# A mixture of experts with two results per token: numbering and loading them in a low and a high block, with VectorE adding x and the high result

## The chip, the cores and the metric

One core of a Trainium2 chip (trn2). A time is the device time of one execution in microseconds; a version is judged by the median of its runs. Engines: PE is TensorE (PEld its weight loads), DVE is VectorE, ACT is ScalarE, POOL is GpSimd, SP is SyncE, which only issues transfers here. An engine's own instruction queue is written SPq, POOLq and so on.

## What is computed

`x` is 2048 tokens of 128 features in float32. The block is a "macaron": half a mixture-of-experts FFN, a causal linear attention, and the same FFN again.

```python
x = x + 0.5 * ffn(layernorm(x))
x = x + attention(layernorm(x))
x = x + 0.5 * ffn(layernorm(x))

def ffn(x):                                   # 8 experts, the best 2 for each token
    top_w, top_i = top_k(x @ Wg, 2)
    top_w = softmax(top_w)
    for i in range(8):                        # w[..., i] is top_w where i was chosen, else 0
        h = gelu(x @ W1[i] + b1[i])           # 128 -> 512
        results += w[..., i] * (h @ W2[i] + b2[i])
```

## The kernel before

**Tiles.** The 2048 tokens are NT = 16 tiles of 128, handled at the end of each FFN in NC = 4 chunks of CH = 4 tiles. Each token has two results, so an FFN has 4096 of them, in NL = 32 tiles of 128 "slots". Slots are sorted by expert, and within an expert by token tile. A tile that two experts share is computed once for each, so an FFN works through NS = 39 items. The program does everything twice where a helper has the argument `f` (0 for the first FFN, 1 for the second), with the attention between.

**Routing (L758 to L924).** VectorE ranks the eight logits of each token, counts the tokens of each expert and gives each of a token's two choices its slot (`picked`, `pos_i`, L803 to L806), the first half of `pos_i` for the best expert (rank 0) and the second for the next (rank 1). From that TensorE builds two tables by slot: `src_row`, the token that a slot belongs to, and `pair_row` (L870), the row of the DRAM tensor `y_rows` in which the slot's result goes: two times the token plus the rank. The weights of the two ranks are `half_w`. Last on VectorE in this stage comes `landed_no` (L916 to L924): for the chunks 0 to 2, up to which count each of four scatter semaphores must have come so that all results of the chunk have been scattered. EARLY = 3 is the number of these chunks.

**Experts.** For each item TensorE computes the hidden layer (L1156) and, one item later, the output (L1165); ScalarE does the gelu (L626) and VectorE the masked sum into `y_back` (L941). GpSimd gathers the rows of each slot tile (L465) and, eight items behind, scatters each finished tile to `y_rows` (L482), on four semaphores in turn; a scatter waits for the one four before it.

**SyncE in an FFN (L336 to L373).** Its queue is in this order: the normalized rows to DRAM (L347), the 39 loads of the first layer's weights as their buffers come free (L355), then for the chunks 0 to 2 twelve reads of `landed_no` into registers (L367), and last, for each chunk, four waits on scatters (L371) and one load of 512 KB from `y_rows` into `y_back` (L372). A chunk's load waits only for the scatters up to its own last result; the last chunk waits for all.

**The end of an FFN.** TensorE puts into a PSUM bank for each chunk the bias (`mix_bias`, L1199), then x by an identity matmul for each tile (`mix_start`, L1204), then the rank-0 results by a matmul with a diagonal matrix of their weights (`mix`, L1129; the diagonals come from ScalarE during the experts, L631). A `mix` waits for the chunk's load. TensorE does the `mix_start` of chunk c + 1 ahead of the `mix` of chunk c; the last `mix` comes after the first tile of the attention has been turned and projected. VectorE (`combine`, L977) adds the bank and the rank-1 results with their weights into x, chunk by chunk. In the first FFN it takes each chunk's moments (L971) and, after chunk 0, the variance; GpSimd computes the root (L492), VectorE the shift (L753, after chunk 1), ScalarE normalizes the first tile of the attention (`xa`, L665), TensorE turns and projects it (L1251, L1259). The first prefix matmul (L1283) comes behind eight warming matmuls (L1062) and writes the banks 0 to 2, so it also waits for all of `combine`. In the second FFN SyncE stores each chunk of x to the output (L377).

```python
landed = [[sp.value_load(landed_no[P - 1:P, c, r:r + 1], ...) for r in range(LANDED)] for c in range(EARLY)]   # L367
for c in range(NC):
    for r in range(LANDED):
        sp.wait_ge(scattered[r], landed[c][r] if c < EARLY else 16 * (NL // LANDED) * (f + 1))                 # L371
    sp.dma_start(y_back[:, c * CH:(c + 1) * CH, :, :], back_rows[:, c * CH:(c + 1) * CH, :, :])                # L372
```

Of the kernel before, what the change touches and what calls it, by code (L numbers as in the profile page):

```python
# [27 lines left out]
P = 128  # L28
# [10 lines left out]
def macaron_kernel(nc, x_d, xT_d, Wa, ba, Wg, W1b, W2, b2, out_d):  # L39
# [38 lines left out]
    EARLY = T // P // 4 - 1  # L78
    assert D == P and NS % RING == 0 and WEIGHTS % RING == 0 and WEIGHTS % ACTS == 0 and T & (T - 1) == 0

    with ExitStack() as ctx:
# [95 lines left out]
        last_slot = sb("last_slot", [P, EARLY])  # L177
        landed_sum = sb("landed_sum", [P, EARLY, LANDED], I32)
        landed_no = sb("landed_no", [P, EARLY, LANDED], I32)
        residue = sb("residue", [P, EARLY, LANDED])  # L180
# [5 lines left out]
        picked = sb("picked", [P, TOPK, NT, E])  # L186
# [22 lines left out]
        y_back = sb("y_back", [P, NT, TOPK, P])  # L209
        xg = y_back[:, :, :, :].rearrange("p t k d -> p (t k) d")  # L210
        y_sum = y_back[:, :, :, :].rearrange("p t k d -> p (t k d)")
# [58 lines left out]
        y_loaded = [sem(f"y_loaded{c}") for c in range(NC)]  # L270
# [22 lines left out]
        def mix_bank(c): return banks[:, (1, 2, 0, 3)[c], :]  # L293
# [31 lines left out]
        def _(sp):  # L325
# [10 lines left out]
            for f in range(2):  # L336
# [25 lines left out]
                for i in range(NS // WEIGHTS * WEIGHTS, NS):  # L362
                    stage(i, i % WEIGHTS)
                back_rows = y_rows[f].rearrange("(p t k) d -> p t k d", k=TOPK, p=P)

                sp.wait_ge(landed_ready, f + 1)
                landed = [[sp.value_load(landed_no[P - 1:P, c, r:r + 1], min_val=16, max_val=32 * NL // LANDED)  # L367
                           for r in range(LANDED)] for c in range(EARLY)]
                for c in range(NC):
                    for r in range(LANDED):  # L370
                        sp.wait_ge(scattered[r], landed[c][r] if c < EARLY else 16 * (NL // LANDED) * (f + 1))  # L371
                    sp.dma_start(y_back[:, c * CH:(c + 1) * CH, :, :],  # L372
                                 back_rows[:, c * CH:(c + 1) * CH, :, :]).then_inc(y_loaded[c], 16)  # L373
# [8 lines left out]
        def _(pool):  # L382
# [25 lines left out]
            g.iota(residue[:, :, :], pattern=[[0, EARLY], [-P, LANDED]], base=4 * P - 1, channel_multiplier=0, **flt).then_inc(consts, 1)  # L408
# [158 lines left out]
        def _(act):  # L567
            s = nc.scalar

            def ffn(f):  # L570
# [59 lines left out]
                def weights(t):  # L630
                    s.activation(diag[:, t, :], ident[:, :], ACT.Copy, scale=half_w[:, 0, t:t + 1]).then_inc(diag_ready, 1)  # L631
# [7 lines left out]
                act.wait_ge(half_ready, f + 1)  # L639
# [85 lines left out]
        def _(dve):  # L725
# [32 lines left out]
            def gate_and_route(f):  # L758
# [35 lines left out]
                if f == 0:  # L794
# [8 lines left out]
                link(v.tensor_tensor(picked[:, :, :, :], is_rank[:, :, :, :],  # L803
                                     slot[:, :, :].unsqueeze(1).to_broadcast([P, TOPK, NT, E]), ALU.mult))
                with nc.allow_low_precision(reason="whole numbers below 2 ** 24, summed in float32"):
                    link(v.tensor_reduce(pos_i[:, :], picked[:, :, :, :].rearrange("p k t e -> p (k t) e"),  # L806
                                         AX.X, ALU.add))
# [47 lines left out]
                for k in range(3, len(HOTS[f])):  # L855
# [14 lines left out]
                v.scalar_tensor_tensor(out=pair_row[:, :], in0=src_row[:, :], scalar=float(TOPK),  # L870
                                       in1=back_bank[:, NL:2 * NL], op0=ALU.mult, op1=ALU.add).then_inc(pair_ready, 1)
# [44 lines left out]
                v.tensor_tensor(last_slot[:, :], slot[:, CH - 1:EARLY * CH:CH, E - 1], chosen[:, CH - 1:EARLY * CH:CH, E - 1],  # L916
                                ALU.add).then_inc(last_ready, 1)
                dve.wait_ge(last_ready, 2 * f + 1)
                v.scalar_tensor_tensor(out=landed_sum[:, :, :], in0=last_slot[:, :].unsqueeze(2).to_broadcast([P, EARLY, LANDED]),
# [46 lines left out]
            def combine(f):  # L966
# [5 lines left out]

                for c in range(NC):
                    dve.wait_ge(mix_ps, NC * f + c + 1)
                    dve.wait_ge(y_loaded[c], 16 * (f + 1))
# [79 lines left out]
        def _(pe):  # L1055
# [77 lines left out]
            def experts(f):  # L1133
# [85 lines left out]
                for c in range(NC):  # L1219
                    mix_bias(c)  # L1220
# [144 lines left out]
```

## Time and profile before

| | us |
|---|---|
| median of 3 runs | 310.52 (310.47 to 310.52) |
| the profiled execution | 308.35 |
| its span, first to last instruction | 306.2 |
| PE busy | 275.5 (90%) |
| DVE busy | 163.3 (53%) |
| ACT busy | 176.4 (58%) |
| POOL busy | 194.9 (64%) |
| mean granted TensorE clock | 0.937 |

The profiled execution has 2.15 us around its span. All start times in the rows are from the span's start. By stages: up to about 30 us the loads and the routing of the first FFN, from 30 to 106 its experts, to about 122 its end, to 195 the attention, to 214 the second routing, to 291 the second experts, and to 306 the end. Register reads, waits and the issue of a transfer are not counted as busy; they show only where one asks for their line.

### The profile page before, as it was taken

Reading aid. Unit: us, or ns where it says so; the run is one execution under the profiler, and the core shown is the slowest. Engines: PE = TensorE matmul, PEld = TensorE weight load, DVE = VectorE, ACT = ScalarE, POOL = GpSimd, SP = SyncE. Lnnn points to the kernel's source line nnn. Section 1 sums busy time; section 2 is a strip of 40 time slices with the busy share of each in tenths; the row PEclk is TensorE's granted clock in tenths of the full one; section 3 lists DMA queues with packets and bytes.
Section 4 is the critical chain, followed back from the end, with each engine's and each line's share of the span. In section 5 each row is a group of like instructions: output and inputs, shape, how many; then the busy total and the mean of one; then the engine's idle time right before and its main releaser. Section 6 shows DMA issues by size and latency. Waiting matters only on the chain.

```text
span 306.2 us, 8012 instructions
## 1 busy us (share of the span) xinstructions
PE 275.5 (90%) x2028; PEld 236.2 (77%) x2033; DVE 163.3 (53%) x557; ACT 176.4 (58%) x643; POOL 194.9 (64%) x256
## 2 busy tenths in 40 slices
PE   8765999999999968989999999576999999999964
PEld 5432999999999956657777776433899999999954
DVE  1789222222222237799999999999222232222214
ACT  2793488887676603353555463384488887676400
POOL 7234777777777622786678878244777777776620
PEclk9576699999999999999999999776699999999999
DMA  5983767666675172000000000021866767675175
GB/s 176 307 273 94 223 190 198 187 193 192 192 213 163 47 230 104 1 0 2 0 2 3 0 0 36 1 104 55 236 188 190 192 191 190 200 208 160 47 255 183
DMA packets 22407, 41.53 MB, mean 136 GB/s; under 512 B 3937, under 2 KB 5985, under 8 KB 22370
## 3 DMA queue, kind: packets, MB, share of 16 engines
q1 hardware_dynamic: 18274, 32.68, 36.5%
q0 software_dynamic: 4096, 8.40, 9.0%
q8 instruction: 19, 0.31, 0.4%
q14 instruction: 18, 0.15, 0.1%
HBM read 33.72 MB, written 7.34 MB: 134 GB/s over the span
## 4 chain that ended last, share of the span: by engine, by line
PE 61%; DVE 12%; DMA 10%; issue 5%; POOL 5%; ACT 4%; SPq 1%; DVEq 0%; POOLq 0%; ACTq 0%
PE banks L1156 22%; PE banks L1165 20%; PE banks L1283 5%; DMA y_back<-y_rows 3%; PE banks L1173 3%; PE banks L1259 2%; DVE prod L1006 2%; DVE local L1010 2%; POOL y_rows L482 2%; DMA x<-in_x_tiles 2%; DMA y_back<-xn_rows,src_row 2%; ACT diag L582 2%; POOL kv L505 2%; PE banks L1285 2%; ACT rows_sb L588 1%
## 5 line engine op out<-in xcount | busy, mean ns | idle before, releaser
L626 ACT ACTIVATE h_act<-banks,w1b 128x128 f32<-128x128 f32 x312 | 89.1, 376 | 12.3 <-PE banks L1156 12.3
L1156 PE MATMUL banks<-rows_sb,w1b 128*128 (+1 forms) x624 | 87.0, 285 | 1.2 <-ACT rows_sb L609 1.2
L941 DVE SCALAR_TENSOR_TENSOR y_back<-banks,own_item,y_back 128x128 f32 x78 | 27.4, 351 | 110.2 <-PE banks L1165 110.2
L465 POOL DMA_INDIRECT y_back<-xn_rows,src_row x64 | 61.6, 963 | 32.4 <-issue 15.9
L1165 PE MATMUL banks<-w,h_act 128*128 (+1 forms) x624 | 81.8, 275 | 0.0
L1156 PEld LDWEIGHTS banks<-rows_sb,w1b 128*128 128x128 f32 x624 | 79.8, 200 | 2.1 <-issue 2.0
L482 POOL DMA_INDIRECT y_rows<-y_back,pair_row x64 | 62.7, 980 | 22.5 <-issue 11.9
L1165 PEld LDWEIGHTS banks<-w,h_act 128*128 128x128 f32 x624 | 75.6, 192 | 0.0
L505 POOL TENSOR_TENSOR kv<-qk,vx 128x1024 f32<-128x1024 f32 x16 | 31.5, 1969 | 16.4 <-DVE qk L963 16.4
L609 ACT COPY rows_sb<-banks 128x128 f32<-128x128 f32 x64 | 16.5, 266 | 34.8 <-PE banks L1173 34.0
L1283 PE MATMUL banks<-kv,tri 128*128 128x384 f32 x64 | 24.8, 510 | 2.0 <-POOL kv L505 2.0
L1006 DVE TENSOR_TENSOR prod<-banks,qk 128x1152 f32<-128x1152 f32 x16 | 21.6, 1352 | 2.8 <-PE banks L1287 2.7
L1010 DVE TENSOR_REDUCE local<-prod 128x144 f32<-128x1152 f32 x16 | 21.6, 1353 | 0.5
L1062 PE MATMUL banks<-blank 128*128 128x512 bf16 x52 | 18.4, 502 | 2.6 <-DVE blank L994 1.2
L1173 PE MATMUL banks<-ident,y_back 128*128 128x128 f32 x64 | 17.9, 292 | 2.6 <-DMA y_back<-xn_rows,src_row 1.9
L931 DVE TENSOR_TENSOR y_back<-blank 128x128 bf16 (+1 forms) x64 | 18.2, 284 | 0.0
L1283 PEld LDWEIGHTS banks<-kv,tri 128*128 128x128 f32 x64 | 10.9, 189 | 9.1 <-POOL kv L505 4.2
L675 ACT ACTIVATE neg<-banks 128x256 f32<-128x256 f32 x16 | 6.1, 383 | 18.7 <-PE banks L1259 18.7
L977 DVE SCALAR_TENSOR_TENSOR x<-y_back,half_w,banks 128x128 f32<-128x128 f32 x32 | 8.9, 343 | 13.9 <-PE banks L1129 13.9
L1062 PEld LDWEIGHTS banks<-blank 128*128 128x128 bf16 x57 | 6.6, 125 | 10.9 <-issue 6.8
L688 ACT COPY mT<-banks 128x128 f32<-128x128 f32 x16 | 4.2, 265 | 18.3 <-PE banks L1264 18.3
L665 ACT ACTIVATE xa<-x,shift,rstd 128x128 f32<-128x128 f32 x16 | 8.0, 507 | 10.7 <-DVE shift L756 10.7
(207 smaller groups left out, 403.0 us busy)
## 6 DMA issues: line engine op xcount, KB each, us to landing
w1b<-in_W1b SPq DMA_DIRECT2D x78, 258.0 KB
y_back<-y_rows SPq DMA_DIRECT2D x8, 512.0 KB, 5.0
xn_rows<-rows_sb SPq DMA_DIRECT2D x8, 256.0 KB, 2.4
rows_sb<-in_x_T SPq DMA_DIRECT2D x4, 256.0 KB, 4.1
x<-in_x_tiles SPq DMA_DIRECT2D x4, 256.0 KB, 6.6
y_back<-xn_rows,src_row POOLq DMA_INDIRECT x64, 3.4
y_rows<-y_back,pair_row POOLq DMA_INDIRECT x64
out<-x SPq DMA_DIRECT2D x4, 256.0 KB, 2.3
```

Source lines behind the costliest of these rows:

```text
L465: g.indirect_dma_start(out=xg[:, n, :], out_offset=None, in_=xn_rows[f][:, :], in_offset=bass.IndirectOffsetOnAxis(ap=src_row[:, n:n + 1], ...
L482: g.indirect_dma_start(out=y_rows[f][:, :], out_offset=bass.IndirectOffsetOnAxis(ap=pair_row[:, i:i + 1], axis=0), in_=xg[:, i, :], in_off ...
L505: g.tensor_tensor(o4, k4, v4, ALU.mult).then_inc(kv_sb, 1)
L626: ins = s.activation(h_act[:, i % ACTS, c * P:(c + 1) * P], h_bank(i % RING)[:, c * P:(c + 1) * P], ACT.Gelu_apprx_tanh, bias=w1b[:, i % W ...
L941: v.scalar_tensor_tensor(out=total, in0=y_bank(r), scalar=own_item[:, bass.ds(i, 1)], in1=total, op0=ALU.mult, op1=ALU.add).then_inc(y_sb, 1)
L1006: v.tensor_tensor(prod[:, :].rearrange("p (b e n) -> p b e n", b=3, n=P), prefix_bank.rearrange("p b (e n) -> p b e n", n=P), q4, ALU.mult ...
L1010: v.tensor_reduce(local[:, :, :].rearrange("p e h -> p (e h)"), prod[:, :].rearrange("p (g d) -> p g d", d=DH), AX.X, ALU.add).then_inc(lo ...
L1062: mm(banks[:, bank, :], blank[:, 0:P], blank[:, :], start=True, stop=True)
L1156: last = mm(h_bank(r)[:, c * P:(c + 1) * P], w1b[:, q, c * P:(c + 1) * P], xgT[:, bass.ds(at[i][0], P)], start=True, stop=True)
L1165: last = mm(y_bank(r), h_act[:, a, c * P:(c + 1) * P], w2[:, bass.ds(col + c * P, P)], start=(c == 0), stop=(c == FC - 1))
L1173: pe.transpose(xg_bank(n), xg[:, n, :], ident[:, :]).then_inc(xg_ps, 1)
L1283: mm(prefix_bank[:, b, :], tri[:, :], kv[:, r, b * n:(b + 1) * n, :].rearrange("p e n -> p (e n)"), start=True, stop=True)
```

## The change

A token's two results are told apart by the number of the expert, no longer by rank. "High" is the one with the larger slot (the higher expert), "low" the other. `y_rows` becomes two blocks of 2048 rows, first all low results, then all high ones; `pair_row` is 2048 times the side plus the token. Since slots are sorted by expert, a low result is never of expert 7 and a high one never of expert 0.

- The positions: `picked` is made once for both choices; the high slot is its maximum, the low slot its sum less that.
- New on VectorE, behind the routing: masks of the two sides, and from them `side_w`, the weights by side (in place of `half_w` in the combine and in ScalarE's diagonals, which now wait for `side_ready`). `last_slot` has the last slot of expert 6 and of expert 7 for each chunk, `landed_no` 8 x 4 counts in place of 3 x 4.
- SyncE reads 16 counts, issues four loads of the low block (256 KB each), reads 12 more counts, and issues four loads of the high block.
- The identity matmuls are gone. VectorE adds x to each bank in one operation over 128x512, once TensorE has written the biases of all four (`bias_ps`); TensorE's `mix` of the low results waits for that (`x_added`) and for the low load; the combine adds the high results.
- All four `mix` come at the end of the experts, the last one no longer behind the first tile of the attention.

```diff
                 sp.wait_ge(landed_ready, f + 1)
-                landed = [[sp.value_load(landed_no[P - 1:P, c, r:r + 1], ...)
-                           for r in range(LANDED)] for c in range(EARLY)]
+                low = [landed_counts(0, c) for c in range(NC)]
                 for c in range(NC):
-                    for r in range(LANDED):
-                        sp.wait_ge(scattered[r], landed[c][r] if c < EARLY else 16 * (NL // LANDED) * (f + 1))
-                    sp.dma_start(y_back[:, c * CH:(c + 1) * CH, :, :], ...).then_inc(y_loaded[c], 16)
+                    load_side(0, c, low[c], low_loaded[c])
+                high = [landed_counts(1, c) for c in range(NC - 1)] + [[16 * (NL // LANDED) * (f + 1)] * LANDED]
+                for c in range(NC):
+                    load_side(1, c, high[c], high_loaded[c])
...
+                def load_side(k, c, landed, loaded):
+                    for r in range(LANDED):
+                        sp.wait_ge(scattered[r], landed[r])
+                    sp.dma_start(y_back[:, k, c * CH:(c + 1) * CH, :],
+                                 back_rows[:, k, c * CH:(c + 1) * CH, :]).then_inc(loaded, 16)
+                def landed_counts(k, c):
+                    return [sp.value_load(landed_no[P - 1:P, c * SIDES + k, r:r + 1], ...) for r in range(LANDED)]
...
-                link(v.tensor_tensor(picked[:, :, :, :], is_rank[:, :, :, :], slot[...].to_broadcast([P, TOPK, NT, E]), ALU.mult))
-                    link(v.tensor_reduce(pos_i[:, :], picked[...], AX.X, ALU.add))
+                link(v.tensor_tensor(picked[:, :, :], chosen[:, :, :], slot[:, :, :], ALU.mult))
+                    v.tensor_reduce(pos_i[:, NT:], picked[:, :, :], AX.X, ALU.max).then_inc(dve_step, 1)
+                    link(v.tensor_reduce(both_pos[:, :], picked[:, :, :], AX.X, ALU.add))
+                link(v.tensor_tensor(pos_i[:, 0:NT], both_pos[:, :], pos_i[:, NT:], ALU.subtract))
...
+                link(v.tensor_tensor(is_side[:, 1, :, :], picked[:, :, :], pos_i[:, NT:]..., ALU.is_equal))
+                link(v.tensor_tensor(is_side[:, 0, :, :], chosen[:, :, :], is_side[:, 1, :, :], ALU.subtract))
+                dve.wait_ge(w_all_ready, f + 1)
+                link(v.tensor_tensor(side_pair[:, :, :, :], is_side[:, :, :, :], w_all[...]..., ALU.mult))
+                v.tensor_reduce(side_w[...], side_pair[...], AX.X, ALU.add).then_inc(side_ready, 1)
...
+                dve.wait_ge(bias_ps, f + 1)
+                for c in range(NC):
+                    v.tensor_tensor(mix_bank(c), mix_bank(c), x[:, c * CH:(c + 1) * CH, :]..., ALU.add).then_inc(x_added, 1)
+                dve.wait_ge(side_ready, f + 1)
                 for c in range(NC):
                     dve.wait_ge(mix_ps, NC * f + c + 1)
-                    dve.wait_ge(y_loaded[c], 16 * (f + 1))
+                    dve.wait_ge(high_loaded[c], 16 * (f + 1))
...
             def mix(f, c):
-                pe.wait_ge(y_loaded[c], 16 * (f + 1))
+                pe.wait_ge(low_loaded[c], 16 * (f + 1))
+                pe.wait_ge(x_added, NC * f + c + 1)
...
-                mix_start(0)
+                last.then_inc(bias_ps, 1)
                 pe.wait_ge(diag_ready, NT * (f + 1))
-                for c in range(1, NC):
-                    mix_start(c)
-                    mix(f, c - 1)
+                for c in range(NC):
+                    mix(f, c)
```

## Rows read from the trace of the kernel before

**Rows 1.** The chain that ended last, end of the first FFN: start us, us, what

```profile
110.30 4.31 DMA y_back<-y_rows
...
117.34 0.50 ACT xa L665
...
123.72 1.29 PE banks L1283 x4
```

**Rows 2.** The same chain, end of the second FFN

```profile
290.64 2.23 DMA y_rows<-y_back,pair_row
...
302.72 0.78 DVE x L977 x3
```

**Rows 3.** L367 on SyncE's queue by FFN: count, ns min/median/max, first and last start

```profile
L367 SPq TENSOR_LOAD <-landed_no x12: 272/278/398, 94.9 to 101.4; - x12
...
L367 SPq TENSOR_LOAD <-landed_no x12: 272/279/412, 278.7 to 285.1; - x12
```

**Rows 4.** SyncE's loads of y_back: timeline of 109 to 111, then L372 in all

```profile
110.30 0.81 SPq L372 DMA_DIRECT2D y_back<-y_rows  x2
...
L372 SPq DMA_DIRECT2D y_back<-y_rows x8: 319/328/1607, 106.0 to 295.9; - x8
```

**Rows 5.** Timeline of GpSimd: scatter of tile 27 (first FFN), tile 28 (second)

```profile
102.04 0.97 POOL L482 DMA_INDIRECT y_rows<-y_back,pair_row  x1 [0.30 <-DVE y_back L941]
...
287.58 0.97 POOL L482 DMA_INDIRECT y_rows<-y_back,pair_row  x1 [0.42 <-DVE y_back L941]
```

**Rows 6.** The page's transfers: count, KB each, median us from issue to landing

```profile
xn_rows<-rows_sb SPq DMA_DIRECT2D x8, 256.0 KB, 2.4
```

**Rows 7.** Timeline of VectorE and GpSimd, end of the first FFN

```profile
111.23 1.12 DVE L977 SCALAR_TENSOR_TENSOR x<-y_back,half_w,banks 128x128 f32<-128x128 f32 x4 [4.14 <-PE banks L1129]
...
114.36 1.05 POOL L492 TENSOR_TENSOR rstd<-var,minus_half 128x4 f32<-128x4 f32 x1 [5.28 <-DVE var L748]
...
115.85 1.12 DVE L977 SCALAR_TENSOR_TENSOR x<-y_back,half_w,banks 128x128 f32<-128x128 f32 x4 [1.57 <-PE banks L1129]
```

**Rows 8.** Timeline of TensorE's bias matmuls; L1006 on VectorE (ns min/median/max)

```profile
106.53 1.14 PE L1199 MATMUL banks<-b_blk,w_allT 32*128 32x512 f32 x8
...
290.32 1.14 PE L1199 MATMUL banks<-b_blk,w_allT 32*128 32x512 f32 x8
...
L1006 DVE TENSOR_TENSOR prod<-banks,qk x16: 1339/1356/1358, 125.7 to 191.1; 128x1152 f32<-128x1152 f32 x16
```

**Rows 9.** Stretches: length, busy PE, PEld, DVE, ACT, POOL, granted clock, DMA, GB/s

```profile
113.00:114.00 1.00, 0.00 (x0) 0.00 (x0) 0.90 (x8) 0.00 (x0) 0.00 (x0) 1.00 1.01 389
192.00:196.00 4.00, 1.15 (x8) 0.59 (x7) 3.83 (x12) 0.99 (x4) 0.02 (x1) 0.99 0.01 2
196.00:197.00 1.00, 1.00 (x4) 0.91 (x4) 0.99 (x8) 0.10 (x1) 0.00 (x0) 0.50 0.00 0
30.00:35.00 5.00, 4.29 (x18) 3.90 (x19) 1.59 (x7) 1.75 (x7) 3.78 (x5) 0.50 0.91 261
35.00:36.00 1.00, 1.00 (x9) 1.00 (x8) 0.00 (x0) 0.50 (x3) 0.69 (x2) 0.75 0.69 118
```

**Rows 10.** TensorE at either clock: projection, a matmul of its shape, warming matmuls

```profile
118.64 0.91 PE L1259 MATMUL banks<-w_fold,xaT 128*128 128x384 f32 x2 [0.35 <-ACT xaT L672]
...
13.94 1.65 PE L1089 MATMUL banks<-w_attn,center 128*128 128x384 f32 x2
...
L1062 PE MATMUL banks<-blank x7: 379/379/379, 122.0 to 123.3; 128*128 128x512 bf16 x7
...
L1062 PE MATMUL banks<-blank x4: 634/634/634, 200.9 to 202.1; 128*128 128x512 bf16 x4
```

**Rows 11.** Timeline of VectorE: the positions in the second routing

```profile
201.42 0.67 DVE L803 TENSOR_TENSOR picked<-is_rank,slot 128x256 f32<-128x256 f32 x1
202.12 0.42 DVE L806 TENSOR_REDUCE pos_i<-picked 128x32 int32<-128x256 f32 x1
```

**Rows 12.** Timeline of VectorE: its first output of the second experts

```profile
221.37 0.35 DVE L941 SCALAR_TENSOR_TENSOR y_back<-banks,own_item,y_back 128x128 f32 x1 [5.23 <-PE banks L1165]
```

More of the change, by code:

```diff
@@ L176, in macaron_kernel @@
         place = sb("place", [P, NS, 2], I32)
[L177 to L180, printed above, removed]
+        last_slot = sb("last_slot", [P, NC, SIDES])
+        landed_sum = sb("landed_sum", [P, NC * SIDES, LANDED], I32)
+        landed_no = sb("landed_no", [P, NC * SIDES, LANDED], I32)
+        residue = sb("residue", [P, NC * SIDES, LANDED])
         expert_i = sb("expert_i", [P, NS], I32)
@@ L185, in macaron_kernel @@
         slot = sb("slot", [P, NT, E])
-        picked = sb("picked", [P, TOPK, NT, E])
+        picked = sb("picked", [P, NT, E])
+        both_pos = sb("both_pos", [P, NT], I32)
+        is_side = sb("is_side", [P, SIDES, NT, E])
+        side_pair = sb("side_pair", [P, SIDES, NT, E])
+        side_w = sb("side_w", [P, SIDES, NT])
         pos_i = sb("pos_i", [P, TOPK * NT], I32)
@@ L269, in macaron_kernel @@
         y_ps, y_sb = map(sem, ("y_ps", "y_sb"))
-        y_loaded = [sem(f"y_loaded{c}") for c in range(NC)]
+        low_loaded = [sem(f"low_loaded{c}") for c in range(NC)]
+        high_loaded = [sem(f"high_loaded{c}") for c in range(NC)]
+        bias_ps, x_added = sem("bias_ps"), sem("x_added")
+        side_ready = sem("side_ready")
         xa_sb, xa_ps, xaT_sb, qkv_ps = map(sem, ("xa_sb", "xa_ps", "xaT_sb", "qkv_ps"))
@@ L638, in ffn @@
                 step(2)
-                act.wait_ge(half_ready, f + 1)
+                act.wait_ge(side_ready, f + 1)
                 for t in range(NT):
@@ L869, in gate_and_route @@
                 dve.wait_ge(table_ready, f + 1)
-                v.scalar_tensor_tensor(out=pair_row[:, :], in0=src_row[:, :], scalar=float(TOPK),
-                                       in1=back_bank[:, NL:2 * NL], op0=ALU.mult, op1=ALU.add).then_inc(pair_ready, 1)
+                v.scalar_tensor_tensor(out=pair_row[:, :], in0=back_bank[:, NL:2 * NL], scalar=float(T),
+                                       in1=src_row[:, :], op0=ALU.mult, op1=ALU.add).then_inc(pair_ready, 1)
                 dve.wait_ge(item_step, done[0])
@@ L1126, in mix @@
             def mix(f, c):
-                pe.wait_ge(y_loaded[c], 16 * (f + 1))
+                pe.wait_ge(low_loaded[c], 16 * (f + 1))
+                pe.wait_ge(x_added, NC * f + c + 1)
                 for t in range(c * CH, (c + 1) * CH):
-                    last = mm(mix_bank(c)[:, (t % CH) * P:(t % CH + 1) * P], diag[:, t, :], y_back[:, t, 0, :],
+                    last = mm(mix_bank(c)[:, (t % CH) * P:(t % CH + 1) * P], diag[:, t, :], y_back[:, 0, t, :],
                               start=False, stop=True, skip_group_check=True)
@@ L1198, in mix_bias @@
                     rows = slice(c * CH * E, (c + 1) * CH * E)
-                    mm(mix_bank(c), w_allT[rows, :], b2_blk[rows, :], start=True, stop=False, skip_group_check=True)
-                def mix_start(c):
-                    for t in range(c * CH, (c + 1) * CH):
-                        mm(mix_bank(c)[:, (t % CH) * P:(t % CH + 1) * P], ident[:, :], x[:, t, :],
-                           start=False, stop=False, skip_group_check=True)
+                    return mm(mix_bank(c), w_allT[rows, :], b2_blk[rows, :], start=True, stop=False, skip_group_check=True)
                 step(0)
@@ L1312, in _ @@
             project(0)
-            mix(0, NC - 1)
             turn_x(1)
@@ L1327, in _ @@
             experts(1)
-            mix(1, NC - 1)
 _INS = ['x_tiles', 'x_T', 'W_attn', 'b_attn', 'L0_ffn_Wg', 'W1b', 'L0_ffn_W2', 'b2_blk']
```

40 lines of the change are left out of this document (22 added, 18 removed).

## The prediction

> **What bounds the kernel now.** I read the chain of waits first, at the ends of the two FFN stages, because everything the change moves lies there. At the end of the first FFN the chain goes through a load of y_back that takes 4.31 us after its issue at 110.30, and then reaches the first normalized tile of the attention (xa at 117.34) and the first prefix matmul (123.72) [rows 1]. At the end of the second it goes through the landing of a scatter (2.23 us), a load and the last additions on VectorE, which end at 302.72 + 0.78 = 303.50 [rows 2]. So both ends hang on when the y_back loads are issued and how long they take. SyncE issues them, so I looked next at what SyncE itself does: its register reads of landed_no, which the page counts in no busy time. There are twelve per FFN; in the first they start from 94.9 to 101.4, one every (101.4 - 94.9) / 11 = 0.59 us, in the second from 278.7 to 285.1, one every 0.58 us [rows 3]. In the kernel before they are hidden: the first load can't be issued before tile 28 or 29 of the results has landed anyway.
>
> **The change part by part.** *SyncE.* The twelve reads become 28: sixteen ahead of the low loads and twelve more between the low loads and the high loads. SyncE does one thing after another, so the high loads are queued behind all 28, and VectorE's combine waits for them. Two loads without a wait are issued 0.81 - 0.33 = 0.48 us apart (two of them span 0.81, the median of one is 0.33) [rows 4].
>
> First FFN: sixteen reads from 94.9 end at 94.9 + 16 x 0.59 = 104.3. The low loads need tiles 24, 25, 26 and 27 (my count of the given inputs' routing: the last expert-6 row of each chunk of four token tiles; the high loads need 28, 29, 30, 31). Tile 27 is scattered at 102.04 [rows 5] and lands 2.2 us later, at 104.2. So all four low loads go out at once, 104.4 to 106.3. Twelve reads more: 106.3 + 7.1 = 113.4. The high loads follow at 113.45, 113.9, 114.4 and 114.9, although the last scatter has landed by 110.3. A high load is 256 KB. The rows have 2.4 us for 256 KB in the other direction [rows 6] and 4.31 for 512 KB in this one, the first of three in a row [rows 1]. I take 2.7, near the row of equal size, and keep 2.4 and 4.3 as ends. Chunk 0 is then there at 116.15. In the kernel before its additions start at 111.23, and the way from there over the moments to GpSimd's root ends at 114.36 + 1.05 = 115.41, after 4.18 us [rows 7]; xa followed only at 117.34, since VectorE did chunk 1 in between (115.85 + 1.12 = 116.97) and then two small operations, some 0.4 us. After the change chunk 1 fits under those 4.18 us. So the root ends at 116.15 + 4.18 = 120.33, and xa starts some 0.4 us later, at 120.75: 3.4 us later than 117.34.
>
> Second FFN: sixteen reads from 278.7 end at 278.7 + 9.3 = 288.0. The low loads need tiles 24, 25, 27, 28, the high ones 29, 30, 30, 31. Tile 28 is scattered at 287.58 [rows 5] and lands at 289.8. The last low load is issued then, SyncE is free at 290.2, twelve reads take 7.0, and the high loads start at 297.25. Chunk 0 is there at 299.95, and VectorE needs 16 x 0.26 = 4.2 us for the four chunks (one every (1.12 - 0.34) / 3 us; four take 1.12 [rows 7]). It ends at 304.2 against 303.50: 0.7 us later. The output store behind it is unchanged.
>
> *TensorE and VectorE.* The 16 identity matmuls that added x go, and VectorE adds x to the four banks instead, as soon as TensorE has written the bias: at 106.53 + 1.14 = 107.7, and at 290.32 + 1.14 = 291.5 [rows 8]. An operation over 128x1152 with one input in PSUM takes 1.36 us [rows 8]; for 128x512 that is 0.6 us, for four 2.4 to 2.7. They end at 110.3 and 294.1, before any high load is there, so they cost nothing; without that cover they would cost 2.5 us in each FFN. The mix matmuls are done about 111.3 and 295 and leave the chain.
>
> *The clock.* In the first FFN TensorE then has nothing to do from about 111.3 until the transpose of xa at 121.4. In the kernel before that stretch was filled with mixes. The granted clock stayed at 1.00 where that stretch still had a hole (113 to 114: 0.00 busy); after 192 to 196, in which TensorE was busy for 1.15 us of 4, it stood at 0.50, which is 1.2 GHz; in the first experts it stood at 0.50 from 30 to 35 though TensorE was busy for 4.29 us of these 5, and rose between 35 and 36 [rows 9]. So I expect the attention to begin at 1.2 GHz. What lies on its way to the first prefix matmul then: the two projections, 0.91 at the full clock and 1.65 for the same shape at half (+0.75 each); eight warming matmuls, starting every 0.21 us at the full clock, every 0.4 at half (+1.6); two transposes (+0.2 each) [rows 10]. Together 3.5 us, and about 2.4 more if the first prefix (2 us of matmuls) still runs slow. Ends: 0 and 5.9. I take the middle, 3.0, since the rise should fall somewhere among the warming matmuls.
>
> *Edits at little or nothing.* The positions: picked is 128x128 instead of 128x256 (0.67), and the one reduction of 0.42 becomes two of half the size and a subtraction over 16 columns [rows 11]. I reckon 1.0 in place of 1.1, that is 0, between -0.3 and +0.3; in the first FFN it is hidden behind ScalarE's squares. The new side weights add five VectorE operations, some 1.6 us, ahead of the experts. Behind them stand VectorE's first clear and output, and ScalarE's wait for side_ready stands ahead of its fourth item. VectorE idles 5.23 us before its first output at 221.37 [rows 12], and ScalarE comes to its wait later still; if that cover were gone, 1.6 us would be lost in each FFN. Scatters that meet low loads land later, but GpSimd waits only for the fourth scatter back, 4 x 1.27 = 5.1 us [rows 5], against a landing of 2.2.
>
> *Sum:* 3.4 + 3.0 + 0.7 = 7.1 us. The profiled execution took 308.35 (span 306.2 and 2.15 around it), so 315.45 there; the median of the runs is 310.52, 2.17 above it, and becomes 317.6.
>
> The Trainium skill, in "Runtime: NRT & Kernel Launch", section "Instruction fetch mechanics", gives about 200 ns for one TENSOR_LOAD of a register. Here the load alone has a median of 278 ns, and a whole read (with its check) 0.58. With 0.2 us for a read, the 28 would take 5.6 us instead of 16.4, and the time would be that of rival B.
>
> **Rivals.** *A: the clock stays up.* For it: the hole at 113 to 114 passed without a fall. Against it: the new one is four times as long as that hole in whole (some 2.5 us), and 192 to 196, with more work in it, ended in a fall. Then 310.52 + 4.1 = 314.6.
>
> *B, faster: the reads don't hold the high loads up.* The point from which it decides: without the clock the reads cost 3.4 + 0.7 = 4.1 us in all, over 28 + 12 reads that the high loads wait for, so 0.1 less for a read, 0.48 us, would make the ends even; below that the change wins. Or SyncE would have to do them earlier. Then the high loads leave with the scatters (about 106, and 295 for the last), VectorE starts on chunk 0 when its additions of x end at 110.2 instead of 111.23, chunk 1 isn't in the way of xa (114.85 instead of 117.34: -2.5), and the second FFN ends 4.2 us after 294.1, at 298.3 instead of 303.5 (-5.2). That gives 302.8. Against it: 24 reads of the same form in the trace, all at 0.58 to 0.59.
>
> *C, slower still:* four loads issued at once can hold SyncE (one of the eight took 1.6 us to issue [rows 4]), the high loads may need 4.3 us to land, and the prefix may still run at 1.2 GHz. With the clock's 5.9 and 1.6 more at each end it is 310.5 + 3.4 + 5.9 + 0.7 + 3.2 = 323.7; I don't expect all of it at once.
>
> **How the numbers follow.** The forecast 0.62; A 0.17; B, or half of it, 0.12; C beyond 321.5 0.09. The range runs from 313.5 (A with landings of 2.4 us) to 321.5 (the forecast with most of C); B is left out, as is the end of C. Faster by over 0.2% (about what a measurement of this kernel can tell) holds B: 0.11; within 0.2%, a B that breaks even, 0.03; slower 0.86.
>
> **What would show it.** Right: 28 reads at 0.58 us; the first high load issued near 113.5 and 297.2; xa near 120.75; the granted clock at 0.50 about 118 to 126; the last scatter landed some 3 us before the first high load. Wrong: the high loads issued within 1 us of their scatters (B), or a clock of 1.00 through the gap (A). If VectorE's additions of x were what its first chunk waits for, the reads would not matter.

## The result, and the profile after

The changed kernel takes 320.22 us (319.07 to 321.77, four runs) against 310.50 (310.03 to 310.52) of the kernel before on the same chip: 1.0324 times as long, interval 1.0283 to 1.0365. The prediction said 317.6, with a range of 313.5 to 321.5. The profiled execution took 321.77, with a span of 320.0.

The chain that ended last, the change's first end. It answers to [rows 1]. SPq is SyncE's queue, L381 is the line of its register reads and L377 that of its loads of y_back:

```profile
103.75 2.20 DMA y_rows<-y_back,pair_row
106.00 0.33 SPq L377
...
107.84 0.28 SPq L381
...
114.78 0.15 SPq L381
...
115.16 3.25 DMA y_back<-y_rows
118.53 1.14 DVE x L1008 x4
...
123.21 0.50 ACT xa L682
...
132.97 1.29 PE banks L1308 x4
```

Between the last low load (107.48) and the first high load (115.16) stands one read after another. Before, this place in the chain held only a load. The same chain at the second end, answering to [rows 2]:

```profile
298.24 4.31 DMA y_rows<-y_back,pair_row
302.56 0.32 SPq L377
...
302.93 0.34 SPq L381
...
309.85 3.06 DMA y_back<-y_rows
313.03 1.01 DVE x L1008 x4
...
315.98 1.29 DVE x L1008 x5
```

Here SyncE first waits for a scatter (4.31 us), then sends the last low load, then reads for 6.9 us. In the share of the chain by engine, SPq was 1% of the span before and is 4% here, and DMA went from 10% to 7%: the chain's wait has moved from transfers to the queue that issues them.

The reads and loads in all (count, ns min/median/max, first and last start), and the landing of the loads, answering to [rows 3, 4]:

```profile
L381 SPq TENSOR_LOAD <-landed_no x56: 272/276/359, 96.7 to 309.2; - x56
...
L377 SPq DMA_DIRECT2D y_back<-y_rows x16: 319/320/344, 106.0 to 311.3; - x16
...
DMA to landing us min/median/max: 3.1/3.8/4.3
```

VectorE and TensorE around the bias of the first FFN, by their timelines, answering to [rows 7, 8]:

```profile
108.28 1.14 PE L1231 MATMUL banks<-b_blk,w_allT 32*128 32x512 f32 x8
109.49 2.49 DVE L1001 TENSOR_TENSOR banks<-banks,x 128x512 f32<-128x512 f32 x4 [0.66 <-PE banks L1231]
110.33 3.81 PE L1161 MATMUL banks<-y_back,diag 128*128 128x128 f32 x32 [0.92 <-DVE banks L1001]
118.53 1.12 DVE L1008 SCALAR_TENSOR_TENSOR x<-y_back,side_w,banks 128x128 f32<-128x128 f32 x4 [6.54 <-DMA y_back<-y_rows]
```

The additions of x end at 111.98 and the mixes at 114.14, and then both engines wait for a high load. What the clock did meanwhile (stretch and length in us, busy PE, PEld, DVE, ACT, POOL, granted clock, DMA share, GB/s), answering to [rows 9]:

```profile
117.00:118.00 1.00, 0.00 (x0) 0.00 (x0) 0.00 (x0) 0.00 (x0) 0.00 (x0) 1.00 0.83 227
118.00:120.00 2.00, 0.00 (x0) 0.00 (x0) 1.44 (x6) 0.00 (x0) 0.00 (x0) 0.80 1.01 364
120.00:124.00 4.00, 0.16 (x1) 0.18 (x1) 3.70 (x21) 0.79 (x2) 1.05 (x1) 0.50 0.14 53
124.00:128.00 4.00, 2.45 (x5) 1.03 (x5) 2.56 (x11) 1.36 (x6) 0.27 (x1) 0.50 0.01 2
128.00:132.00 4.00, 4.00 (x10) 1.57 (x10) 2.83 (x15) 1.39 (x5) 2.94 (x3) 0.50 0.02 6
132.00:134.00 2.00, 2.00 (x7) 1.21 (x6) 0.00 (x0) 0.00 (x0) 2.00 (x2) 0.79 0.00 0
```

TensorE's granted clock goes from 1.00 (2.4 GHz) to 0.50 (1.2 GHz) during the wait, and the attention begins at 0.50.

For a comparison by stages I take these marks from each trace: the first bias matmul of each FFN, xa, the first prefix matmul, and the end of VectorE's last addition. The table has the differences between them in us. The ratio is the time against the kernel before on the same chip; the runs came from several chips, so kernels are compared by their ratios. The experiments are told below.

| kernel | bias 1 at | bias 1 to xa | xa to prefix | prefix to bias 2 | bias 2 to end | ratio |
|---|---|---|---|---|---|---|
| before | 106.53 | 10.81 | 6.38 | 166.60 | 13.18 | 1 |
| after | 108.28 | 14.93 | 9.76 | 168.01 | 16.29 | 1.0324 |
| e1_const | 107.21 | 8.28 | 8.76 | 165.64 | 11.98 | 0.9848 |
| e2_before28 | 106.03 | 15.73 | 6.37 | 165.54 | 18.47 | 1.0230 |
| e3_warm | 106.08 | 14.84 | 8.82 | 167.04 | 15.00 | 1.0144 |
| e4_ahead | 106.24 | 10.12 | 9.15 | 165.90 | 12.37 | 0.9918 |
| e5_const_ident | 108.66 | 10.57 | 8.71 | 167.56 | 11.26 | 1.0026 |
| e6_early | 107.32 | 9.55 | 8.91 | 168.03 | 11.20 | 1.0004 |
| e7_early_warm | 107.41 | 8.30 | 6.29 | 168.74 | 11.15 | 0.9931 |
| e8_thin | 107.87 | 14.76 | 9.76 | 166.91 | 14.96 | 1.0206 |
| e9_const_warm | 106.14 | 9.60 | 6.29 | 167.43 | 10.37 | 0.9801 |

From before to after the three stages that the change touches grow by 4.12, 3.38 and 3.11: 10.6 us. The rest of the 13.77 us by which VectorE ends later in the profiled pair (317.27 against 303.50) is 1.75 at the start of the program and 1.41 in the attention and the second experts. The medians are only 9.7 apart, so these 3.2 us can't all belong to the change: the profiled execution of before lay 2.2 below its median, that of after 1.6 above its own. The column at the start varies from 106.03 to 108.66 with no order in it. The fourth varies from 165.54 to 168.74; the two kernels without the change's router have 166.60 and 165.54, the other nine a median of 167.43. From VectorE's first output to the bias, the second experts take 68.95 before (290.32 - 221.37) and 69.02 after (300.98 - 231.96), so the 1.41 does not lie there. Whether the change adds some tenths in the second routing stays open.

### The profile page after: what moved, and what is told of

Read it like the earlier page. It is cut to its first block, busy times and chain, and to the rows that moved or that the text cites. A ratio compares the mean times of both kernels' runs of the same rounds, so it can differ in the third digit from the quotient of the medians.

```text
span 320.0 us, 8039 instructions
## 1 busy us (share of the span) xinstructions
PE 276.7 (86%) x1969; PEld 234.0 (73%) x1969; DVE 171.1 (53%) x577; ACT 176.7 (55%) x643; POOL 195.1 (61%) x256
## 4 chain that ended last, share of the span: by engine, by line
PE 57%; DVE 14%; DMA 7%; issue 7%; POOL 7%; SPq 4%; ACT 2%; DVEq 0%; POOLq 0%; ACTq 0%
PE banks L1188 19%; PE banks L1197 17%; PE banks L1308 5%; POOL y_rows L499 4%; SPq L381 3%; PE banks L1284 3%; PE banks L1205 2%; PE banks L1093 2%; DVE prod L1037 2%; DVE local L1041 2%; DMA y_back<-xn_rows,src_row 2%; PE banks L1104 2%; DMA y_rows<-y_back,pair_row 2%; DMA y_back<-y_rows 2%; DVE x L1008 2%
## 5 line engine op out<-in xcount | busy, mean ns | idle before, releaser
L1197 PEld LDWEIGHTS banks<-w,h_act 128*128 128x128 f32 x624 | 76.5, 194 | 0.0
L1093 PE MATMUL banks<-blank 128*128 128x512 bf16 x57 | 23.3, 584 | 1.2 <-DVE blank L1025 1.2
L1093 PEld LDWEIGHTS banks<-blank 128*128 128x128 bf16 x57 | 7.4, 140 | 13.0 <-issue 10.3
L1008 DVE SCALAR_TENSOR_TENSOR x<-y_back,side_w,banks 128x128 f32<-128x128 f32 x32 | 8.7, 343 | 14.9 <-DMA y_back<-y_rows 14.9
L1284 PE MATMUL banks<-w_fold,xaT 128*128 128x384 f32 x32 | 14.7, 545 | 1.7 <-DVE qk L989 1.2
L682 ACT ACTIVATE xa<-x,shift,rstd 128x128 f32<-128x128 f32 x16 | 8.0, 506 | 14.8 <-DVE shift L773 14.8
```

Source lines behind the costliest of these rows:

```text
L1093: mm(banks[:, bank, :], blank[:, 0:P], blank[:, :], start=True, stop=True)
L1197: last = mm(y_bank(r), h_act[:, a, c * P:(c + 1) * P], w2[:, bass.ds(col + c * P, P)], start=(c == 0), stop=(c == FC - 1))
L1284: mm(qkv_bank, xaT[:, i % 2, :], wqkv, start=True, stop=True).then_inc(qkv_ps, 1)
```

## The experiments

Two theories stood against each other. *Reads:* the 28 register reads in SyncE's queue hold the high loads up, and the clock falls in the gap they leave; without them the change would win. *Rival:* what costs is elsewhere, in the additions of x on VectorE, in more and smaller loads, or in the later scatters.

**e1_const: the reads away.** SyncE waits on constants which hold for these inputs; the sixteen loads, the order and everything else stay.

```diff
-                low = [landed_counts(0, c) for c in range(NC)]
+                low_tiles = ((25, 26, 27, 28), (25, 26, 28, 29))[f]
+                high_tiles = ((29, 30, 31, 32), (30, 31, 31, 32))[f]
                 for c in range(NC):
-                    load_side(0, c, low[c], low_loaded[c])
-                high = [landed_counts(1, c) for c in range(NC - 1)] + [...]
+                    load_side(0, c, tiles_landed(low_tiles[c]), low_loaded[c])
```

> The changed kernel without the 28 register reads of landed_no in each FFN: SyncE waits on constants, which are the counts that these inputs' routing gives (low 25, 26, 27, 28 tiles and high 29, 30, 31, 32 in the first FFN; 25, 26, 28, 29 and 30, 31, 31, 32 in the second), so each load waits for the same scatters as before. Theory 'reads' (the high loads are late because SyncE reads registers ahead of them): the first high load leaves with tile 28's landing instead of 7 us and more after the last low load; xa some 7 us earlier, no fall of the clock in the gap, the second end some 8 us shorter; 302 to 306 us in all, faster than the kernel before. Rival 'adds and halves' (what holds the end is VectorE's additions of x, or the loads of 256 KB in 2 KB pieces themselves): 317 to 320, as now.

Measured: 306.73 us, ratio 0.9848 (0.9787 to 0.9908). Against the 1.0324 of after, the reads are worth 0.0476 x 310.5 = 14.8 us, more than the whole loss (12.0 of it in the three stages of the table: 6.65, 1.00 and 4.31). The time is 0.7 above the range that the reads give and 10 below the rival's; by the ratio it is 0.9848 x 310.5 = 305.8, inside that range. In its chain at the first end the high load is no longer there; VectorE's additions of x lead to its first chunk:

```profile
108.42 2.02 DVE banks L1004 x4
...
110.82 1.12 DVE x L1011 x4
...
115.49 0.50 ACT xa L685
...
121.69 2.56 PE banks L1096 x8
124.25 1.29 PE banks L1311 x4
```

This end comes 2.53 us earlier than before by its distance from the bias (8.28 against 10.81). xa to the prefix is still 8.76, since the clock falls in the hole before xa here too: the eight warming matmuls of L1096 take 2.56 where e7 below has 1.73. So the fall of the clock does not need the reads, against what was expected. The second end is 4.31 shorter than in after, not 8: there the loads now wait for late scatters. The rival of e1 falls.

**e2_before28: the reads alone.** The kernel before, with sixteen reads more in each FFN (28 in all), whose values nothing uses.

```diff
+                for n in range(16):
+                    sp.value_load(landed_no[P - 1:P, n % EARLY, n % LANDED:n % LANDED + 1], ...)
```

> The kernel before with 16 more register reads of landed_no behind its twelve (28 in all, results not used), nothing else changed. Theory 'reads': the first load leaves at 94.9 + 28 x 0.59 = 111.4 instead of 106.0 in the first FFN and at 295.0 instead of 291.65 in the second; some +4 us and +1 us, and up to 3 more if TensorE's hole then lets the clock fall: 315 to 319. Rival 'adds and halves': reads alone cost nothing that counts, 310 to 311.

Measured: 318.38 us, ratio 1.0230 (1.0161 to 1.0299). None of the change is in it, and it is 2.3% slower. The first load leaves at 110.66 instead of 106.04, and in the second FFN at 298.50 instead of 291.65, each time behind the added reads (L370). Of the second 6.85 us, 3.35 had come about before that end; counted from the bias, the load is 5.1 later in the first FFN and 3.5 in the second:

```profile
109.62 0.28 SPq L370
...
110.66 4.04 DMA y_back<-y_rows
...
297.81 0.27 SPq L370
298.50 3.89 DMA y_back<-y_rows
```

Thus the reads cost by themselves, and at both ends. In this kernel the mixes lie behind the loads: the clock stood at 0.50 from 114 to 120 and was back at 1.00 from 122 on, with xa at 121.76, so that xa to the prefix took 6.37, as before.

**e3_warm: the gap filled.** After, with 40 warming matmuls on TensorE between the last mix and the first transpose.

```diff
             pe.wait_ge(y_sb, NS)
+            keep_warm(40)
             turn_x(0)
```

> The changed kernel with 40 warming matmuls (0.21 us each at the full clock, 8.6 us) on TensorE behind its last mix of the first FFN, where it idles for 10 us. Theory: the granted clock stays at 1.00 there, and xa to first prefix takes 6.4 us as in the kernel before instead of 9.8; xa itself stays where it is; 316 to 317.5. Rival 'the clock's fall is covered by other waits': 319 to 320.5.

Measured: 316.84 us, ratio 1.0144 (1.0053 to 1.0235). The time lies in the expected range, but not for the expected reason: the clock stays up through the gap and falls behind it. Stretches of e3, columns as above:

```profile
118.00:120.00 2.00, 2.00 (x11) 0.90 (x10) 1.86 (x13) 0.00 (x0) 0.63 (x1) 1.00 0.19 70
120.00:122.00 2.00, 0.91 (x4) 0.22 (x2) 1.84 (x10) 1.05 (x3) 0.42 (x1) 1.00 0.01 4
122.00:124.00 2.00, 1.02 (x3) 0.44 (x3) 1.51 (x8) 1.00 (x5) 0.00 (x0) 0.92 0.00 0
124.00:126.00 2.00, 1.54 (x3) 0.82 (x4) 1.97 (x8) 0.11 (x1) 1.51 (x1) 0.50 0.00 0
```

From xa on TensorE works in short pieces between ScalarE and VectorE, 0.91 and 1.02 us of two each time, and the clock falls there. xa to the prefix is 8.82, 0.9 less than after's 9.76 and still 2.4 more than before: filling the gap alone gives back about a quarter of what the clock cost. The time fell by more than that, 0.018 x 310.5 = 5.6 us; of this the trace shows 1.0 at the first end (23.66 against 24.69 from bias to prefix), 1.3 at the second, where a scatter landed in 3.11 instead of 4.31, and the rest ahead of the first bias and in the fourth column. I put no weight on the rest.

**e4_ahead: fewer reads, all in front.** The four low loads share the last low chunk's counts, and the high counts are read ahead of all loads: sixteen reads in place of 28.

```diff
-                low = [landed_counts(0, c) for c in range(NC)]
-                for c in range(NC):
-                    load_side(0, c, low[c], low_loaded[c])
+                low = landed_counts(0, NC - 1)
                 high = [landed_counts(1, c) for c in range(NC - 1)] + [...]
                 for c in range(NC):
+                    load_side(0, c, low, low_loaded[c])
+                for c in range(NC):
                     load_side(1, c, high[c], high_loaded[c])
```

> The changed kernel with 16 reads in place of 28, all ahead of the low loads: four counts of the last low chunk, for which all low loads wait, and the twelve of the high chunks. Theory 'reads': sixteen reads end near 104.4 in the first FFN and 288 in the second, about when tile 27 lands, and the high loads follow the low ones with no reads between: 303 to 307, faster than the kernel before. Rival 'adds and halves': 317 to 320.

Measured: 308.60 us, ratio 0.9918 (0.9881 to 0.9954): faster than before, above the expected range. The miss is in the transfers. The four low loads leave one behind the other from 104.03, and scatters that land beside them are slow; now they and the loads set both ends (and with 9.15 from xa to the prefix the clock falls here too):

```profile
103.50 4.20 DMA y_rows<-y_back,pair_row
107.71 3.85 DMA y_back<-y_rows
...
291.73 4.89 DMA y_rows<-y_back,pair_row
...
296.75 3.75 DMA y_back<-y_rows
```

**e5_const_ident: x again by TensorE.** e1, with the sixteen identity matmuls of the kernel before in place of VectorE's four additions, but all of them ahead of the first mix; the kernel before had only those of two chunks there.

```diff
-                dve.wait_ge(bias_ps, f + 1)
-                for c in range(NC):
-                    v.tensor_tensor(mix_bank(c), mix_bank(c), x[...], ALU.add).then_inc(x_added, 1)
...
+                for t in range(NT):
+                    mm(mix_bank(t // CH)[...], ident[:, :], x[:, t, :], start=False, stop=False, ...)
```

> e1_const with x added as in the kernel before, by 16 identity matmuls on TensorE behind the biases, and no addition of x on VectorE. Theory: with the reads gone the four additions of x (2.5 us) are what VectorE's first chunk of the first FFN waits for (its first operation came at 110.82, right behind them), so the first end gains up to 1 us and the second nothing: 305.5 to 306.7. Rival 'the additions cost their 2.5 us at both ends': 302 to 303. Rival 'TensorE's 4 us of identity matmuls come back into the chain': 308 or more.

Measured: 309.98 us, ratio 1.0026 (0.9982 to 1.0070), against 0.9848 of e1. My theory missed and the rival held. All 32 pieces of the sixteen matmuls stand between the bias and the first mix, and VectorE waits behind the mixes:

```profile
109.73 3.84 PE L1246 MATMUL banks<-x,ident 128*128 128x128 f32 x32
113.40 3.74 PE L1159 MATMUL banks<-y_back,diag 128*128 128x128 f32 x32
```

The first chunk begins 114.55 - 108.66 = 5.9 us after the bias, in e1 110.82 - 107.21 = 3.6. So against sixteen matmuls in one block, VectorE's additions gain 2.3 us at the first end once the reads are gone. In the order of the kernel before some half of the 3.84 us would stand behind the first mix (an estimate), which would leave a few tenths of this gain; that was not run. Nor does the first end explain the whole 5.5 us between the two ratios (0.0178 x 310.5): the second end is 0.7 shorter than in e1, and the rest lies ahead of the first bias and in the fourth column.

**e6_early: real reads, moved.** The twelve high reads stand ahead of the loop that loads the last weights; two low chunks share their counts (eight reads after it).

```diff
+                sp.wait_ge(landed_ready, f + 1)
+                high = [landed_counts(1, c) for c in range(NC - 1)] + [...]
                 with sp.Fori(1, NS // WEIGHTS) as j:
...
-                low = [landed_counts(0, c) for c in range(NC)]
+                low = [landed_counts(0, c) for c in range(1, NC, 2)]
```

> The changed kernel with its reads moved and fewer, no constants: the twelve of the high chunks ahead of SyncE's loop over the weight loads, and eight of the low chunks (two chunks share the counts of the later one) where all were. Theory: eight reads from about 94.9 end at 99.6 and at 283.4, ahead of tile 24's landing, so loads leave as in e1_const; the twelve early reads hide in the weight loads' lead: 306 to 308. Rival 'twelve reads ahead of the loop make the weight loads late': TensorE waits for w1b in the experts, 310 or more.

Measured: 309.80 us, ratio 1.0004 (0.9961 to 1.0047), about 2 us above the expected range. The ends are earlier than before (9.55 from bias to xa, 11.20 at the second), but the clock falls (8.91 to the prefix) and the fourth column is 1.4 us longer. The rival holds in part: TensorE waits 0.7 us in all for weights (w1b), and in e7, with the same reads, 2.4.

**e7_early_warm: e6 with the chain filled too.** Twelve warming matmuls in the gap, and six between the sparse pieces of the chain behind xa.

```diff
+            keep_warm(12)
             turn_x(0)
+            keep_warm(2)
             project(0)
+            keep_warm(4)
             turn_x(1)
```

> e6_early with 12 warming matmuls behind the last mix of the first FFN, 2 between the first tile's transpose and its projection and 4 behind that. Theory: the clock fell in e1_const and e3_warm because TensorE's chain from xa to phi is sparse, not only for the gap ahead of it; filled, it stays at 1.00, and from xa to the first prefix take 6.4 us instead of 8.6: some 2 us less than e6_early. Rival: the filling delays the transposes by as much as the clock gives, no difference.

Measured: 307.88 us, ratio 0.9931 (0.9889 to 0.9972), 2 us less than e6, as expected. The clock is 1.00 in every stretch of 2 us from 108 to 124; the projection and the warming matmuls take half of what they took in after:

```profile
116.00:118.00 2.00, 1.75 (x7) 0.84 (x8) 1.88 (x8) 0.96 (x4) 0.00 (x0) 1.00 0.08 29
...
117.01 0.85 PE banks L1284 x2
...
120.28 1.73 PE banks L1093 x8
```

xa to the prefix is 6.29, near the 6.38 of before: the clock was all of that stage's loss. Whether the fill of the chain alone would do, without that of the gap, was not run. This kernel reads its counts, so that it works with whatever the routing gives, and it is faster than both kernels. It pays for the early reads elsewhere. In the second FFN they stand on SyncE's queue from 215.8 to 222.5, and the next weight load leaves 8.85 us behind the one ahead of them (223.48 and 214.63). TensorE's wait for weights (us in total, times, longest), which only e6 and e7 of all these traces show:

```profile
PE banks L1188 <- DMA w1b<-in_W1b: 2.4, 2, 1.5
```

That accounts for the 2.1 us by which the fourth column is longer than before.

**e8_thin: low loads with a quarter of the bytes.** Is the slow scatter at the second end due to the low loads beside it? This is the changed kernel with three quarters of the low results left out of its loads.

```diff
+                    n = CH if k else 1
-                    sp.dma_start(y_back[:, k, c * CH:(c + 1) * CH, :], ...)
+                    sp.dma_start(y_back[:, k, c * CH:c * CH + n, :], ...)
```

> The changed kernel with its low loads cut to one of four token tiles (64 KB instead of 256 KB each; three quarters of the low results are left out). Theory: in the second FFN the scatter of tile 28 took 4.3 us to land because three low loads were moving beside it, and the twelve reads wait for it; with thin loads it lands after some 2.3 to 2.8 us and the second end is 1.5 to 2 us shorter, the first end the same: 1.5 to 2 us less than the changed kernel, 318 to 319. Rival: the landing has another cause, 320 as now.

Measured: 317.80 us, ratio 1.0206 (1.0135 to 1.0278). The scatter of tile 28 landed in less:

```profile
297.00 2.60 DMA y_rows<-y_back,pair_row
```

That is 4.31 in after and 3.11 in e3, both with whole low loads. The other late scatters of the traces settle what this one leaves open. From a scatter's issue to the last count on its semaphore, in us, for the tiles 28, 29, 30 and 31 (a few counts are missing from the records):

| kernel | loads of y_back beside them | first FFN | second FFN |
|---|---|---|---|
| e2_before28 | none yet | 2.20, 2.21, 2.24, 2.22 | 2.23, 2.23, 2.23, 2.22 |
| e8_thin | 64 KB each | 2.78, 2.29, 2.23, 2.25 | 2.60, 2.53, 2.29, 2.24 |
| e3_warm | 256 KB each | 3.68, 4.54, 3.47, 2.39 | 3.11, 4.09, 3.61, 2.84 |
| after | 256 KB each | 4.33, 4.64, 3.57, 2.46 | 4.31, 3.89, 2.85, 3.90 |
| before | 512 KB each | 2.23, 4.66, 3.56, 2.45 | 2.83, 2.22, 2.23, 3.95 |

In before the loads stand beside the later ones alone, since the first leaves when tile 28 (second FFN: 29) has landed. In e2, whose first load leaves when all of them have landed, no scatter is slow; with thin loads they lie near that, with whole loads up to 2.4 us above it. So the loads hold the scatters up, and their bytes matter. What this is worth in time is less clear: the second end is 14.96, against 16.29 in after, but e3 has 15.00 without thin loads, and the time fell by more than this stage shows.

**e9_const_warm: both losses gone.** e1 with the fill of e7: rival B in full.

> The kernel of e1 (28 reads of SyncE replaced by constants that hold for these inputs) with the fill of e7 as well: 12 warming matmuls after the last mix of the first FFN, two after the first transpose, four after the first projection. It asks what the change is worth once both of its losses are gone, that is, rival B of the prediction in full (302.8 us). By the theory that the two losses add and are of different places: in e1 xa to the first prefix matmul took 115.49 to 124.25 = 8.8 us with the clock at 0.50, in e7 6.3 us with it at 1.00, so 2.4 us below e1, a ratio to the kernel before of 0.985 - 0.008 = 0.977, some 303.5 to 305. By the rival that e7 gained from something else than the clock, or that e1's gain and the fill's overlap (the fill delays the transpose of xa, which in e1 comes 1.8 us earlier after the mixes than in e7): a ratio of 0.983 or more, and a clock that still falls between 113 and 124.

Measured: 304.43 us, ratio 0.9801 (0.9761 to 0.9842), as expected in time (303.5 to 305) and 0.5% below e1; the two intervals overlap, but the clock is 1.00 in every stretch from 108 to 126 and xa to the prefix is 6.29. The reads and the clock are two losses in two places, and without them the change's idea is worth 2%. At the two ends SyncE now waits for transfers alone:

```profile
103.40 4.04 DMA y_rows<-y_back,pair_row
...
107.45 3.48 DMA y_back<-y_rows
...
289.78 3.01 DMA y_rows<-y_back,pair_row
...
292.93 3.62 DMA y_back<-y_rows
```

## Why the prediction was right, point by point

**The reads: right, to the tenth.** 28 reads in each FFN at some 0.58 us. The first high load was forecast 113.45 - 106.53 = 6.9 us behind the bias and left 115.16 - 108.28 = 6.9 behind it; the last scatter before it had been issued at 109.87. e2 shows the same reads costing 2.3% in the old kernel, e1 that the change without them is faster. The Trainium skill gives about 200 ns for a register load ("Runtime: NRT & Kernel Launch", section "Instruction fetch mechanics"), there from HBM. The loads here, of a tile in SBUF, took 276 ns, and the checked read 0.58 us, so the measurement decides, and the time that rival B would have by that figure did not come. The Trainium skill also puts the floor of a tensor_load at some 600 ns ("DMA: Bandwidth & Descriptors", section "Latency and other measured facts"). The load alone lies under it here with 276 ns; only the whole read, with its check, comes near it.

**The first end: 3.4 forecast, 4.12 measured.** The mis-sized term is the load's landing: 2.7 taken, with 2.4 and 4.3 as ends [rows 1, 6], 3.25 measured. The path behind it was forecast at 4.6 us from landing to xa and took 123.21 - 118.41 = 4.8.

**The additions of x at no cost: right.** 2.49 us for four (2.4 to 2.7 forecast), done at 111.98, 6.5 us ahead of the first chunk. The mixes ended at 114.14, 5.9 behind the bias where the prediction had some 4.8, but they are off the chain. The cover of the additions is the reads; e1 shows them on the chain when the cover goes, as the prediction said, and e5 that there they are still cheaper than sixteen matmuls ahead of the first mix.

**The clock: 3.0 forecast from ends 0 and 5.9, 3.38 measured.** The order was the forecast one: projections 1.65 instead of 0.91, eight warming matmuls 3.41 us instead of e7's 1.73, and the rise during the prefix (0.79 in 132 to 134). The clock stood at 0.50 from 120 to 132, later and longer than the 118 to 126 that were forecast. The forecast let the rise fall among the warming matmuls; it came behind them. So of its two terms the 3.5 for the way at the low clock came almost whole, and the 2.4 for a slow first prefix not at all (1.29, as before); that the middle of the two ends lay near is luck. Rival A (the clock stays up) falls. e3 shows that one part of the reason was not in the prediction: not only the gap, but also the sparse chain behind xa lets the clock fall.

**The second end: 0.7 forecast, 3.11 measured. This is the step that failed.** It took tile 28's landing from the row of 2.23 [rows 2, 5]. Beside the scatter of that row a single load was asked for, 1.2 us before it landed (at 291.65); here three low loads had been asked for since 298.86, 0.6 us behind the scatter, and it took 4.31. The dearer price stood in the trace of before as well. At the end of its first FFN tile 29 was scattered just ahead of the first load, and the second load, which waits for tile 29, left at 110.30 [rows 4], 4.7 us behind that scatter:

```profile
105.58 0.96 POOL L482 DMA_INDIRECT y_rows<-y_back,pair_row  x1 [0.82 <-DVE y_back L941]
...
106.04 0.34 SPq L372 DMA_DIRECT2D y_back<-y_rows  x1
```

What the transfers did in after while tile 27's scatter was under way (104 to 105; it took 2.20) and while tile 28's hung (columns as above, the last two DMA share and GB/s):

```profile
104.00:105.00 1.00, 1.00 (x11) 1.00 (x11) 0.09 (x1) 1.00 (x4) 0.72 (x1) 1.00 0.00 0
...
300.00:301.00 1.00, 1.00 (x14) 0.88 (x12) 0.35 (x1) 0.00 (x0) 0.96 (x1) 1.00 0.89 174
301.00:302.00 1.00, 1.00 (x9) 0.29 (x8) 0.35 (x1) 0.00 (x0) 0.71 (x1) 1.00 0.83 236
```

So the high load left 8.87 us behind the bias instead of 6.93, which is 1.94 of the 2.41 us missed. The other 0.47 lies behind the load's issue: a landing of 3.06 for 2.7, and 4.36 instead of 4.25 from there to the end of the additions. The prediction wrote that scatters which meet low loads land later, and looked only for who on GpSimd waits for that; SyncE waits for it too, with twelve reads behind.

**The sum: 7.1 forecast.** In the profiled pair the three stages add 10.6; by the medians the time grew by 9.7. It stayed inside the range because the range had room for most of rival C, that is, for high loads that take 4.3 us to land and a first prefix at the low clock. Neither came; the late scatter, which the range had no term for, used that room, and that is luck. The 0 for the route holds within what can be seen: in the second routing `picked` took 0.54 for 0.67 [rows 11], the two reductions and the subtraction stand in place of one reduction, and VectorE still idled 5.02 us before its first output, for 5.23 [rows 12].

**Rival B: its mechanism is real, its price was not.** With the reads away e1 came to 306.7 and e9 to 304.4, not 302.8. In e1 the first end was as forecast there (2.53 earlier for 2.5), in e9 half of it (1.21), since tile 28 landed in 4.04. The second end was not: 5.2 forecast, 1.2 (e1) and 2.8 (e9) measured, since the scatter of tile 30 took 4.8 and 3.0 instead of 2.2 (in e1 it was issued at 290.54, and the load that waits for it left at 295.44). And the clock, which B had left out, took 2.4 in e1. **Rival C** did not come: the four high loads did not hold SyncE up (0.34 at most), and they landed in 3.25 and 3.06, not 4.3.

## What to carry to other kernels

Before a transfer is split so that its first part can leave early, look at what its issuer must do between the parts: here 28 reads of 0.58 us stood ahead of the transfers that the end waits for, and with twenty of them, twelve moved ahead of the weight loads, and the clock kept up (e7), a loss of 3% became a gain of 0.7%. Moved reads are not free either: there they made weight loads late. A gap that the change opened on TensorE was paid again behind it by the clock, and filling it gave little back (e3) until the chain behind it was filled as well (e7). And a landing read from a quiet stretch (2.2 us) is no price for a stretch into which the change itself brings transfers (4.3).

## What was not expected of the hardware

The last scatters of 128 rows landed in 2.20 to 2.24 us where no load stood beside them (e2), and those that the chains wait for in 4.31 (after), 4.20 and 4.89 (e4), 4.06 (e6), 3.77 (e7), 4.04 and 3.01 (e9) where loads of y_back moved beside them; with a quarter of the loads' bytes one took 2.60. It isn't these loads alone: one of e3, issued at 284.32 with only weight loads beside it (a DMA share of 0.67 from 284 to 286), took 3.55. Why a load on one queue holds a scatter on another up, no run here shows.

TensorE's clock was still at 1.00 in the empty stretch 117 to 118 of after, and fell in e3 where TensorE had worked without a hole until 120 and then only in short pieces.
